# A two-layer image transformer: per-head folded weights in the second attention

## What is computed

```
def _L1_attn_ref(x, w_qkv, b_qkv, th1, th2, w_out, b_out):
    ...
    qkv = x @ w_qkv + b_qkv
    q, k, v = jnp.split(qkv, 3, axis=-1)
    to_heads = lambda t: t.reshape(b, n, H, DH).transpose(0, 2, 1, 3)
    q, k, v = (to_heads(q), to_heads(k), to_heads(v))
    dots = jnp.einsum('bhnd,bhmd->bhnm', q, k) * scale
    dots = jnp.einsum('gh,bhnm->bgnm', th1, dots)
    attn = jax.nn.softmax(dots, axis=-1)
    attn = jnp.einsum('gh,bhnm->bgnm', th2, attn)
    out = jnp.einsum('bhnm,bhmd->bhnd', attn, v)
    out = out.transpose(0, 2, 1, 3).reshape(b, n, H * DH)
    return out @ w_out + b_out
...
h = h + _L1_attn_ref(_layernorm(h, axis=-1), L1_attn_w_qkv, L1_attn_b_qkv, L1_attn_th1, L1_attn_th2, L1_attn_w_out, L1_attn_b_out)
h = h + _L1_ffn_ref(_layernorm(h, axis=-1), L1_ffn_Wg, L1_ffn_W1, L1_ffn_b1, L1_ffn_W2, L1_ffn_b2)
```

## Time and profile before

| | us |
|---|---|
| time, median of 3 runs (lowest, highest) | 216.32 (215.18, 222.64) |
| span of the profiled execution | 213.6 |
| last matmul of `project(4)` | 166.8 |
| end of the last `slot_ranks(4)` matmul | 171.8 |
| end of the fillers | 181.1 |
| last pair's result on DVE | 199.4 |

### The profile page before, as it was taken

One profiled execution on the slowest core, in us unless ns is written; L12 is line 12 of the kernel. 1 busy time (PEld: TensorE's weight loads), 2 busy tenths in 40 slices (PEclk: granted clock), 3 DMA queues, 4 the chain that ended last, 5 costly groups with the idle time before them and its releaser, 6 DMA issues.

```text
span 213.6 us, 4128 instructions
## 1 busy us (share of the span) xinstructions
PE 182.5 (85%) x1474; PEld 142.6 (67%) x1474; DVE 98.9 (46%) x389; ACT 78.6 (37%) x222; POOL 74.2 (35%) x103
## 2 busy tenths in 40 slices
PE   6999999987998799999967987989999699999200
PEld 2955666876785699999955556779988444777100
DVE  0063386888360133322157505766677670455104
ACT  2003345453417955666001471122375410444100
POOL 8026042301778054455314000000134660477710
PEclk9999999997559999999999999999999859999755
DMA  6959998993111359941130799100001115311142
GB/s 207 280 169 293 367 312 254 333 408 142 48 47 36 84 154 337 370 165 31 41 104 0 264 430 253 40 0 5 0 0 27 48 37 113 57 51 46 43 123 55
DMA packets 17822, 30.83 MB, mean 144 GB/s; under 512 B 5166, under 2 KB 11262, under 8 KB 17418
## 3 DMA queue, kind: packets, MB, share of 16 engines
q1 hardware_dynamic: 14416, 26.84, 39.1%
q0 software_dynamic: 2784, 3.31, 6.0%
q10 hardware_dynamic: 602, 0.42, 0.7%
HBM read 23.49 MB, written 7.11 MB: 143 GB/s over the span
## 4 chain that ended last, share of the span: by engine, by line
PE 74%; DVE 9%; DMA 7%; ACT 5%; issue 3%; POOL 1%; POOLq 1%; ACTq 0%; DVEq 0%; SPq 0%
PE ps L1372 68%; DMA o_tok<-o_rows 3%; DMA o_rows<-o_sb,result_row 2%; PE ps L1742 2%; PE ps L1869 2%; DMA patchesT<-in_patchesT 2%; DVE dots_m L1161 1%; ACT hid_b L739 1%; POOL o_rows L598 1%; PE ps L1382 1%; DVE h L1119 1%; PE ps L1613 1%; ACT L733 1%; ACT L732 1%; POOLq L80 1%
## 5 line engine op out<-in xcount | busy, mean ns | idle before, releaser
L521 POOL TENSOR_TENSOR ln_rstd<-ln_var,minus_half 119x1 f32<-119x1 f32 x12 | 6.7, 560 | 58.3 <-DVE ln_var L876 58.1
L552 POOL DMA_INDIRECT o_rows<-o_sb,result_row x16 | 15.5, 970 | 20.0 <-DVE o_sb L1093 20.0
L739 ACT ACTIVATE hid_b<-ps,w_ring 128x128 f32<-128x128 f32 x64 | 18.1, 365 | 10.8 <-PE ps L1372 10.8
L598 POOL DMA_INDIRECT o_rows<-o_sb,result_row x16 | 15.1, 942 | 13.2 <-DVE o_sb L1343 9.9
L1372 PE MATMUL ps<-w_ring,hid_b 128*128 128x128 f32 x128 | 17.1, 277 | 1.1 <-ACT hid_b L739 1.1
L616 ACT COPY xT<-ps 128x119 f32<-128x119 f32 (+1 forms) x15 | 3.7, 251 | 37.9 <-PE ps L1382 31.6
L1372 PE MATMUL ps<-filler 128*128 128x512 bf16 x50 | 15.6, 467 | 1.5 <-DVE filler L893 1.5
L1372 PE MATMUL ps<-xbT,w_ring 128*128 128x128 f32 x128 | 16.8, 275 | 0.0
L1372 PEld LDWEIGHTS ps<-w_ring,hid_b 128*128 128x128 f32 x128 | 15.5, 192 | 1.5 <-ACT hid_b L739 1.5
L545 POOL DMA_INDIRECT rooms<-xm,room x10 | 11.0, 1098 | 15.6 <-issue 15.6
L1372 PEld LDWEIGHTS ps<-xbT,w_ring 128*128 128x128 f32 x128 | 15.5, 192 | 0.0
(11 more groups left out here) (212 smaller groups left out, 379.5 us busy)
## 6 DMA issues: line engine op xcount, KB each, us to landing
w_ring<-in_w_routed SPq DMA_DIRECT2D x16, 514.0 KB, 6.7
m<-in_m SPq DMA_DIRECT2D x2, 2048.0 KB, 11.1
rooms<-zeros SPq DMA_DIRECT2D x8, 330.0 KB, 5.9
patchesT<-in_patchesT SPq DMA_DIRECT2D x6, 272.0 KB, 4.7
xb<-rooms SPq DMA_DIRECT2D x16, 66.0 KB, 2.1
w_s<-in_w_s SPq DMA_DIRECT2D x2, 512.0 KB, 6.4
moe_b<-in_moe_b SPq DMA_DIRECT2D x2, 512.0 KB, 16.6
rooms<-zeros SPq DMA_DIRECT2D x1, 792.0 KB, 5.9
```

The source lines that it names most:

```text
L521: nc.gpsimd.tensor_tensor(ln_rstd[:, g:g + 1], ln_var[:, g:g + 1], minus_half[:], ALU.pow).then_inc(rstd_ready, 1)
L552: nc.gpsimd.indirect_dma_start(o_rows[:], bass.IndirectOffsetOnAxis(ap=result_row[:, b:b + 1], axis=0), o_sb[:, b, :], None).then_inc(o_sc ...
L598: nc.gpsimd.indirect_dma_start(o_rows[:], bass.IndirectOffsetOnAxis(ap=result_row2[0:past_, j:j + 1], axis=0), o2_sb[0:past_, j, :], None) ...
L739: nc.scalar.activation(hid_b[:, b % RING, c, :], ps[:, b % 2, c * BS:(c + 1) * BS], ACT.Gelu, bias=w_ring[:, b % WRING, FF + c:FF + c + 1] ...
```

## The change

What moves is the second attention's arithmetic, its tiles and its place in the queues. (1) Weights: since the rows of a layer norm sum to zero, feature 127 of `xn` is replaced by 1 and `w_t` (w_qkv turned, with the bias as a column) is centred on DVE, so that biases need no operation. POOL forms `q_mixed` (q weights times `th1`, per head), PE multiplies it with the k weights (`mixed`) into `m_x`, one 128x128 matrix per mixed head; DVE forms `out_mixed` and PE multiplies it with the v weights (`folded`) into `w_f`. (2) Attention: `keys` applies `m_x` to `xT` per head; `dots(b)` takes four images a tile at partition steps of 32, with 8x17 columns; the softmax runs on 128 partitions for two tiles at a time; VectorE turns the probabilities in 32x32 blocks (L1181 of the new kernel); `held` applies them to the tokens themselves (`xq`, stored to DRAM and loaded again at 32-row steps); `project(g)` applies `w_f`, eight matmuls. (3) Queues: `shared_down(0)` moves to the start of the blocks, the exponential of the first routing behind them.

```diff
-SHARED_BANKS = (6, 7, 6, 7, 6)
+SHARED_BANKS = (6, 7, 2, 3, 6)
+EARLY = 1
+A_BANKS = ((2, 3, 6, 7), (1, 2, 3))
+DOTS_BANK = (0, 1, 2, 3)
...
+            for g in range(G):
+                sp.wait_ge(xn_ready, 2 * G + g + 1)
+                sp.dma_start(x_rows[g * GT:g * GT + rows(g), :], xn[0:rows(g), g, :]).then_inc(x_stored, 16)
+            sp.wait_ge(x_stored, 16 * (G + 1))
+            for i in range(PER):
+                sp.dma_start(xq[Q * i:Q * i + Q, :, :], image_rows(i)).then_inc(xq_loaded, 16)
             load("m1", m1[:], dram["m1"])
...
+            nc.gpsimd.memset(probs[:], 0.0).then_inc(probs_zero, 1)
...
+            for c in range(4):
+                nc.gpsimd.tensor_tensor(q_mixed[:, c], w_t[:, c, 0:D].unsqueeze(1).to_broadcast([128, H, D]),
+                                        th1_q[:, c, :].unsqueeze(2).to_broadcast([128, H, D]),
...
-            act.wait_ge(top_shifted, 1)
-            nc.scalar.activation(top_e[:], top_e[:], ACT.Exp).then_inc(top_exp, 1)
-            nc.scalar.activation(warm[:], eps_col[0:1, 0:1], ACT.Gelu)
             for b in range(NB):
...
+            mixed_out(0)
             act.wait_ge(o_scattered, 16 * NB)
             load_rest(act, o_tok, o_rest_loaded)
-            turn_out(2)
+            turn_out(2, (0, 1))
+            mixed_out(1)
+            turn_out(2, (2,))
+            for g in range(H):
+                keys_to(0, g)
+            turn_out(2, (3, 4))
+            exponents(0)
+            exponents(1)
+            folded_out(0)
+            folded_out(1)
+            held_to(0)
+            held_to(1)
+            for g in range(4):
+                keys_to(1, g)
+            held_to(2)
+            for g in range(4, H):
+                keys_to(1, g)
+            held_to(3)
+            exponents(2)
+            exponents(3)
...
             for b in range(NB):
                 block_biased(b)
...
+                if b < EARLY:
+                    shared_joined(b)
+                if 4 <= b < 8:
+                    out_weights(b - 4)
...
+            for g in range(EARLY, G - 1):
+                shared_joined(g)
...
+            def dots(b):
+                for s_ in range(BATCH):
+                    for i in range(PER):
+                        at = S * (PER * (BATCH * b + s_) + i)
+                        last = mm(ps[Q * i:Q * i + Q, DOTS_BANK[b], s_ * H * S:(s_ + 1) * H * S].rearrange(
+                            "p (h m) -> p h m", h=H), xT[:, at:at + Q], keysT[:, :, at:at + S])
+            def held(grp):
+                if grp % BATCH == 0:
+                    pe.wait_ge(probsT_ready, grp // BATCH + 1)
+                if grp >= 1:
+                    pe.wait_ge(held_out, grp)
+                for i in range(PER):
+                    last = mm(ps[:, 4 + i, 0:H * S].rearrange("p (h q) -> p h q", h=H),
+                              xq[Q * i:Q * i + Q, grp, :], probsT[Q * i:Q * i + Q, grp, :, 0:S])
             def project(g):
+                pe.wait_ge(held_out, -(-IMGS * (g + 1) // PER) if g < LAST else GRPS)
-                for c in range(4):
-                    last = mm(ps[0:n, 6, 0:D], aoT[:, g % 2, c, 0:n], w_out[:, c, :], c == 0, c == 3)
+                for hh in range(H):
+                    last = mm(ps[0:n, OUT_BANK, 0:D], heldT[:, hh, cols(g)], w_f[:, hh, :], hh == 0, hh == H - 1)
```

More of the change, by code:

```diff
@@ L1651, in _ @@
             block_ups(0)
+            for g in range(EARLY):
+                shared_down(g)
             for b in range(NB):
@@ L1657, in _, with mixed @@
                 block_downs(b)
-            for g in range(G):
-                shared_down(g)
-            def values(g):
-                if g >= len(V_BANKS):
-                    pe.wait_ge(v_out, g - len(V_BANKS) + 1)
-                mm(ps[0:rows(g), V_BANKS[g % 4], :], xT[:, cols(g)], w_qkv[:, 2 * H * DH:]).then_inc(v_done, 1)
-            here(pe, "w_qkv", "w_out")
-            pe.wait_ge(shared_added, G)
-            for g in range(G):
+            def mixed(half):
+                if half == 0:
+                    pe.wait_ge(q_mixed_ready, 4)
+                for c in range(4):
+                    last = mm(ps[:, half, :], w_t[:, 4 + c, 0:D],
+                              q_mixed[:, c, 4 * half:4 * half + 4, :].rearrange("p g d -> p (g d)"), c == 0, c == 3)
+                last.then_inc(m_done, 1)
@@ L1798, in slot_ranks @@
                 last.then_inc(rank2_done, 1)
+            mixed(0)
+            for g in range(EARLY, G):
+                shared_down(g)
+            mixed(1)
+            for g in range(3):
+                turn_second(g)
+            pe.wait_ge(shared_added, G)
+            pe.wait_ge(m_out, 1)
+            pe.wait_ge(xT_ready, 2 * G + 3)
+            for g in range(H):
+                keys(0, g)
+            turn_second(3)
+            turn_second(4)
+            pe.wait_ge(xT_padded, 1)
+            pe.wait_ge(keys_out, H)
@@ L1822, in _ @@
-            mix2(2)
-            attend(1)
-            mix(4)
+            folded(0)
+            folded(1)
+            pe.wait_ge(xq_loaded, 16 * PER)
+            pe.wait_ge(xT_ready, 3 * G)
+            held(0)
+            held(1)
+            pe.wait_ge(wf_out, 2)
+            project(0)
+            for g in range(4):
+                keys(1, g)
+            held(2)
+            for g in range(4, H):
+                keys(1, g)
+            held(3)
+            pe.wait_ge(keys_out, 2 * H)
```

512 lines of the change are left out of this document (183 added, 329 removed).

## The result

The changed kernel took 223.34 us, median of 4 runs (222.61 to 223.66), the kernel before beside it 216.33 (215.18 to 222.64). The ratio is 1.030, interval 1.023 to 1.037: slower. Ratios compare the faster executions of both kernels and medians take all of them, and the traces of e0, e1, e2, e3, e5 and e10 are of slower executions. The profiled execution has a span of 220.4 against 213.6, +6.8; the forecast span was 219.0.

A forecast was written before the change was run, and what follows sets the result against it. PE was busy almost throughout, filling nearly every rung of the attention ladder; later its fillers' end released the second experts. Terms 1.0 + 3.8 - 1.0 - 2.9 - 4.75 - 6.65 + 8.3 + 7.6 = +5.4: span 219.0, time 221.7, range 213.5 to 227.

The forecast's parts named there:

- Block loop: Expert blocks: shared_down(0) adds 1.8 us on PE where it idled 0.77, so the loop ends 1.03 later.
- If either cover failed the cost would be tenths: Block loop: added DVE and POOL products fit beside PE's work at no cost; otherwise tenths, since the scatters catch up.
- The memset of probs lies in POOL's idle time before the gates; nothing.: First stage, before the gates: clearing probs on POOL was to cost nothing.
- Joining, keys, first half, middle: From the last block to project(1): join +3.8, then shorter join, keys and attention steps, reaching 10.5 us ahead.
- the rival of the early fall: Second attention: clock falls already at 132 to 135, costing 3.8 or 8 more, 225.5 to 229.8; chance 0.13.
- Tail: From project(1) to the last slot_ranks: 25.3 us at full clock where there were 17.0, +8.3.
- Clock: Tail: PE's clock at half from about 148, not back before the fillers; +7.6 us.
- POOL's last scatter ends 5.1 later, still ahead: After the ranks: fillers take the same 9.47, the last scatter ends before them, and everything behind is unchanged.
- the five stages: Start to last hid_s, 69.6; last block, 34.0; project(1), 40.8; slot_ranks(4), 32.9; end of span, 41.8.
- clock holds: Tail rival: the clock stays up, or falls only after project(3); 214.1, up to 217; chance 0.20.
- Faster, since my serial steps overlap: Tail rival: ladder no longer than the old 17 us, DVE answering at once; 207 to 210; chance 0.12.

The follow-up runs named there:

- e0: The changed kernel run once more with no edit, on another chip: 223.19, ratio 1.030 (1.009 to 1.051) to the kernel before.
- e1: The changed kernel with only GpSimd's memset of probs moved up, ahead of the first ln_rstd: 1.002 (0.996 to 1.009) of the kernel before.
- e2: The changed kernel with the four q_mixed products moved from GpSimd to VectorE in blocks 8 to 11: 1.013 (1.007 to 1.018) of the kernel before.
- e3: The changed kernel with 45 filler matmuls in TensorE's gaps from project(1) on, order unchanged: 0.996 (0.990 to 1.001) of the kernel before.
- e5: The changed kernel with tail order changed, fillers in TensorE's gaps, memset of probs moved up and q_mixed on VectorE: median 215.56 (209.76 to 217.26), no interval.
- e10: The kernel before with seven fillers added in its first stage: 223.98 (219.59 to 227.60) against 224.96 unedited, no interval.
- e6: The kernel before with its own memset of xb2 moved up to where the changed kernel has its memset of probs: 1.018 (1.009 to 1.028).

## Why the prediction was right or wrong

The verdict and the time (221.7 for 223.3) were right, and the tail and its clock, which made the loss, were the mechanism that I named. That the number came so near is luck, as the terms below show.

- *Block loop*, +1.03: 34.2 against 33.1, +1.1. Right in size, and partly by luck: "If either cover failed the cost would be tenths" named the scatters as the ones that wait, and it was `result_row`, for 3.27 us, that `shared_down(0)` covered all but 0.2 to 0.6 of.
- *"The memset of probs lies in POOL's idle time before the gates; nothing."* The step that failed. Idle time of GpSimd was the wrong thing to look at; VectorE's `xn` was under way there. It cost 0.8 in the first trace and 1.6 to 2.2 where the clock was back sooner; the 1.5 of half clock behind it in two traces comes on top.
- The rest of the first stage's +5.0 (late patches, a half clock from 14.7) was in no term. It is likelier of the execution than of the change, since e6 has it without the change; my forecast was made against a trace that had not.
- *Joining, keys, first half, middle*: `shared_joined(3)` ahead of the join, which starts 8.9 behind the last block (forecast 9.25); keys at 15.2 (forecast 16.05); two batches of dots in 1.15 (1.2); the turn on VectorE 0.71 (0.7); the copy 0.63 (0.74); `project(1)` at 40.3 (40.8). Right, each step, though two prices were too low: a key matmul at 0.455, where my own row gives 8.14 / 16 = 0.51 and the trace 0.49, and a projection at 1.83 from a row of 1.05 for half of it, which took 2.0. Three traces of eight add 1.7, the rival of the early fall.
- *Tail*, +8.3: 25.0 in e3 against the walk's 25.3. Right.
- *Clock*, +7.6, "not back before the fillers": mis-sized in the first trace, 5.3 for 7.6, since the three projections do bring it back at times; e2's trace shows the forecast's case, 7.8.
- *"POOL's last scatter ends 5.1 later, still ahead" of the fillers.* Wrong, without a price of its own in this sum: it ended 7.7 later, fillers took 8.0 and not 9.5, and the reload's second piece, at 189.40, set the pairs. From the ranks to the end it was 41.0 against 41.8.
- The misses of the five stages, +5.0, +0.3, -0.4, -2.6 and -0.8, make the +1.4 of span. The forecast was right to 0.7% with terms wrong by far more. From the rows, the change's own price is 0.8 to 2.2 (memset) + 1.1 - 11.9 + 13.4 - 0.8 = 2.6 to 4.0, between 1 and 2%, where I forecast 5.4. The rest of the measured 3% is the first stage's late patches and half clock, as far as the two traces tell; the other runs left none. So "slower by more than 2%" was in part luck too: without that stage, by these rows, the change would have come out within 2%.
- *Rivals*: "clock holds" gave 214.1 up to 217; with fillers that made it hold (e3) the time was 0.996 of the kernel before, so the price was about right; the event did not come by itself. "Faster, since my serial steps overlap" was false of the ladder as written; with order and clock mended the tail came to 19.4, not to the rival's 17.

## What to carry to other kernels

Before an instruction is put into an engine's idle time, look at what runs beside it on the others, VectorE beside GpSimd above all: a memset of 1.8 us on GpSimd, which nobody waited for, held a VectorE operation of 0.35 for 3.4. A stage that is turned from dense matrix work into a ladder of small steps pays twice, for the steps and for TensorE's clock; each can be had back by itself, by the order of the queues (5.6 here) and by fillers (5.3). A piece of the chain of waits is a name, not a price: ask what the waiting engine was doing meanwhile.

## What was not expected of the hardware

- A GpSimd product of 1024 elements (1.91) held VectorE's `result_row` of one element for 3.27, over more than one product: by these records VectorE did not get in between two of GpSimd's instructions that stood back to back. The changed kernel's repeat has 2.92, e1 3.07.
- TensorE's clock at the same place of the same instructions is 1.00 in one execution and half in another: `project(0)` took 1.98 or 3.6, the middle stage 40.3 in five traces of kernels with that stage as changed and 42.0 in three. A forecast from one trace has at least that spread, 1.7, at such a place.
- A fall of the clock can come with TensorE's records without a gap from 4 on (e10; it fell just after 16).
